# Four units of v ahead of the last down products, none between the maxima

## What is computed

```python
x = x + attn(layernorm(x))        # 16 heads of 16 channels, causal, rotary on q and k
    # q, k, v = h @ Wq.T, h @ Wk.T, h @ Wv.T ; softmax(q k^T / 4) v ; @ Wo.T
x = x + ffn(layernorm(x))         # silu(gate) * up, then down (hidden 768, integer weights)
x = x + wkv6(layernorm(x))
x = x + ffn(layernorm(x))
```

## Time and profile before

| | us |
|---|---|
| median of 3 runs | 3179.18 |
| lowest, highest | 3177.82, 3183.08 |
| the profiled execution's own time | 3171.1 |
| its span, first to last instruction | 3169.0 |
| mean granted TensorE clock, share of full speed | 0.958 |

### The profile page before, as it was taken

The page is one execution under the profiler, slowest core; times in us unless marked ns, Lnnn a source line. Parts: engine busy times, 40 slices in busy tenths (PEclk is TensorE's granted clock), DMA queues, the critical chain, the costliest instruction groups (busy, mean ns, idle before and its releaser), DMA issues.

```text
span 3169.0 us, 46787 instructions
## 1 busy us (share of the span) xinstructions
PE 2786.1 (88%) x16704; PEld 1732.4 (55%) x16704; DVE 2412.7 (76%) x4581; ACT 1420.5 (45%) x3073; POOL 1439.7 (45%) x1638
## 2 busy tenths in 40 slices
PE   4598989998899998989889998898988989899898
PEld 2235674366644576345763556635565355753667
DVE  7577887777786787867878678786787868877666
ACT  1373434744256433654336542375513744247342
POOL 2134662445624565244643357334563345623464
PEclk7799999999999999999999999899999999999999
DMA  6500143000520125001340012400124001240000
GB/s 161 123 2 9 33 68 75 2 19 24 84 59 2 31 32 94 29 2 30 49 102 4 1 41 41 102 2 2 40 41 102 2 2 40 41 89 2 8 13 15
DMA packets 80135, 128.00 MB, mean 40 GB/s; under 512 B 12443, under 2 KB 66107, under 8 KB 73707
## 3 DMA queue, kind: packets, MB, share of 16 engines
q1 hardware_dynamic: 76611, 123.71, 19.1%
q10 hardware_dynamic: 3264, 0.79, 0.1%
HBM read 75.08 MB, written 33.65 MB: 34 GB/s over the span
## 4 chain that ended last, share of the span: by engine, by line
PE 51%; DVE 24%; POOL 10%; issue 6%; ACT 4%; DMA 2%; SPq 1%; DVEq 0%; POOLq 0%; ACTq 0%
PE PB L1574 7%; PE PB L1505 6%; PE PB L1489 6%; DVE mxp L1141 6%; PE PB L1475 6%; PE PB L1589 5%; DVE arena L1344 4%; DVE arena L1353 3%; PE PB L1671 3%; POOL rstd L597 2%; PE PB L1765 2%; PE PB L1682 2%; PE PB L1426 2%; POOL hl L700 2%; PE PB L1448 2%
## 5 line engine op out<-in xcount | busy, mean ns | idle before, releaser
L853 ACT ACTIVATE arena<-PB 128x512 f32<-128x512 f32 (+3 forms) x1536 | 658.7, 511 | 403.1 <-PE PB L1489 344.4
L1141 DVE TENSOR_REDUCE mxp<-PB 128x1 f32<-128x512 f32 (+3 forms) x1216 | 723.2, 652 | 144.6 <-PE PB L1478 78.9
L1489 PE MATMUL PB<-arena 99*128 99x512 bf16 (+3 forms) x1536 | 443.9, 335 | 69.7 <-DMA arena<-augT 39.8
L1475 PE MATMUL PB<-arena 96*128 96x512 bf16 (+3 forms) x1536 | 458.2, 340 | 50.0 <-DMA arena<-parts 30.7
L700 POOL TENSOR_TENSOR hl<-arena,hh 128x512 fp32r<-128x512 f32 x192 | 251.8, 1315 | 296.9 <-ACT hh L880 295.3
L1505 PE MATMUL PB<-arena 128*32 128x512 f32 (+3 forms) x3072 | 326.1, 498 | 8.5 <-POOL arena L676 8.5
L1475 PEld LDWEIGHTS PB<-arena 96*128 96x128 bf16 x1536 | 150.7, 99 | 279.0 <-ACT arena L853 95.8
L676 POOL TENSOR_SCALAR_AFFINE_SELECT arena<-arena 128x512 f32<-128x512 f32 x256 | 162.7, 638 | 305.4 <-ACT arena L853 275.6
L1489 PEld LDWEIGHTS PB<-arena 99*128 99x128 bf16 x1536 | 138.7, 98 | 288.2 <-DVE mxp L1141 86.0
L1765 PE MATMUL PB<-arena 128*128 128x128 f32 x1792 | 247.0, 292 | 54.9 <-DVE arena L1344 45.7
L1574 PE MATMUL PB<-xh,wgu 128*128 128x512 f32 x768 | 258.4, 418 | 39.2 <-issue 36.0
(11 more groups left out here) (151 smaller groups left out, 5382.7 us busy)
## 6 DMA issues: line engine op xcount, KB each, us to landing
arena<-parts SPq DMA_DIRECT2D x112, 256.0 KB, 10.6
parts<-arena SPq DMA_DIRECT2D x192, 128.0 KB
arena<-parts SPq DMA_DIRECT2D x16, 768.0 KB, 17.9
arena<-in_x SPq DMA_DIRECT2D x16, 512.0 KB, 7.4
arena<-parts SPq DMA_DIRECT2D x16, 512.0 KB, 19.8
xres<-in_x SPq DMA_DIRECT2D x16, 512.0 KB, 4.8
mix_in<-lora_hi SPq DMA_DIRECT2D x128, 64.0 KB, 2.0
out<-xres SPq DMA_DIRECT2D x16, 512.0 KB, 11.8
```

The lines of the kernel that those rows point to most:

```text
L853: act.activation(pt[:, U % 3, h, 0:n], bank(b, "score", t)[:, 0:n], ACT.Exp, scale=DH ** -0.5).then_inc(act_emptied, 1)
L1141: dve.reduce_max(mxp[:, k // 2 % 2, hs[0]:hs[-1] + 1, col:col + 1], bank(b, "max", t)[:, 0:n * len(hs)].rearrange("p (h n) -> p h n", n=n) ...
L1475: last = mm(ps, qst[0:AUG, i // 4, HG * (k // 2) + h, 128 * (i % 4):128 * (i % 4) + 128], kst[0:AUG, s0 // HALF, HG * (k // 2) + h, 0:n], ...
L1489: mm(ps[:, 0:n], kst[0:AUG + 3, j // 4, h, 128 * (j % 4):128 * (j % 4) + 128], qst[0:AUG + 3, f, h, HALF - n:HALF], start=True, stop=True) ...
```

## The change

The plan and PE's list both get all four units of v ahead of the last down products of the second FFN, and in the prologue ahead of the first maximum. The two units at steps 4 and 8 of the maxima are gone. Nothing else is edited: the same products, copies and reductions are done, and ACT's, DVE's, POOL's and SyncE's lists are unchanged.

```diff
-V_AT = (4, 8)
@@ psum_plan, ffn
         elif b + 1 < NB:
-            add(b + 1, "v", (0, 1), "act")
+            add(b + 1, "v", range(4), "act")
         add(b, f"dn{k}", (2, 3), "dve")
@@ psum_plan, prologue
-    add(0, "v", (0, 1), "act")
+    add(0, "v", range(4), "act")
@@ psum_plan, steps of the attention
-            if t in V_AT:
-                add(b, "v", (2 + V_AT.index(t),), "act")
@@ PE, prologue
-                v_item(0, 0)
-                v_item(0, 1)
+                for n in range(4):
+                    v_item(0, n)
@@ PE, steps of the attention
-                        if t in V_AT:
-                            v_item(b, 2 + V_AT.index(t))
@@ PE, ffn
                         elif ahead:
-                            v_item(b + 1, 0)
-                            v_item(b + 1, 1)
+                            for n in range(4):
+                                v_item(b + 1, n)
                         for n in (2, 3):
                             down(n, 0, (NM - 1,))
```

## The result

The changed kernel takes 3217.3 us (median of 4, 3212.98 to 3218.59) against 3181.13 for the kernel before (4 runs): a ratio of 1.0107, 95% interval 1.009 to 1.0124. It is slower by 36.2 us. The direction was forecast; the size was not: 3198.9 was predicted, 19.7 us slower, and 3217.3 lies above the stated range.

A forecast was written before the change was run, and what follows sets the result against it. The prediction took the chain of waits through the seam, then DVE's pace in the maxima, as the bound. Per seam +3.45 + 0.48 - 1.12 = +2.81 us; seven seams, +19.7 on 3179.18, gave 3198.9 us, range 3191 to 3208.

The forecast's parts named there:

- The seam, +3.45: Between sequences, ahead of the last down products: two more units of v delay these by their whole length, +3.45 us a seam.
- the banks of `dn3`: Down products at the seam: `dn3` 2 and 3 wait for later gate and up banks, covered by POOL's low part; cost nothing.
- Rival (b): At the seam: the new units hide in a wait that ends later than read; 3174.7 us, chance 0.03.
- The new wait ahead of the first maximum, +0.48: Behind the seam: maximum 0 waits for ACT to copy v out of its bank, so DVE starts +0.48 us later a seam.
- What comes back between the maxima, -1.12: Among the first maxima: removing two units returns only DVE's idle 0.30 and 0.82 us, since DVE sets the pace; -1.12 a seam.
- Rival (a): Between the maxima: PE's relief comes back in full, 3.56 us a seam instead of 1.12; 3181.8 us, chance 0.06.
- All that follows (maxima, splits, scores) hangs on DVE's progress, so the 1.12 is carried forward: From the first maxima through the scores: DVE's progress sets the pace, so the 1.12 us gained a seam is kept.
- nothing else could use the 3.45 us: At the seam: DVE, ACT and POOL idle until `dn3` banks are filled, so the added 3.45 us serve no other work.
- The first sequence, nothing: In the first sequence, added units and DVE's gain both vanish in waits for transfers of 30.70 and 33.52 us; no change.
- Zero for the clock: Behind the seam: the clock falls earlier, its effect between -3.5 and +4.5 us in all, taken as zero.
- Rival (c): Behind the seam: the clock falls early and is still down when scores and maxima share PE; 3206.8 us, chance 0.13.
- the sign that the prediction gave for (c): Behind the seam: a longer time from first maximum to first join would show the clock returning late; before, 23.2 to 24.4 us.

The follow-up runs named there:

- late_before: Kernel before the change, plus a SyncE wait: loads of the next x start only once the first `augT` transfer has landed; ratio 0.9982 to before, 0.999 repeated.
- late_after: Changed kernel, plus a SyncE wait: loads of the next x start only once the first `augT` transfer has landed; ratio 1.0025 to before, 1.0032 repeated.
- before_again: Kernel before the change, nothing edited, run for a second profile; 3181.94 us (one run).
- spread_stack_late: Against spread: second-half head loads wait for the first `augT` transfer to land, loads of x for the second; 3216.55 us, ratio 1.0091 to the kernel before.
- spread: Against the kernel before: no unit of v at the seam, all four between the maxima at steps 6, 11, 15, 20; 3146.02 us, ratio 0.9894.

## Why the prediction was wrong

**The seam, +3.45: right.** 16.61 became 20.04, +3.43, at every seam. PE was not idle ahead of the last down products, and the banks of `dn3` cost nothing. Rival (b) is out.

**The new wait ahead of the first maximum, +0.48: right,** 0.58 measured, and no idle time behind it.

**What comes back between the maxima, -1.12: right as a mechanism.** The two idle times are gone, and with the loads held back the way to the join is 0.65 us shorter (24.52 and 24.56 in the late_before pair, 23.88 and 23.87 in the late_after pair), where 0.48 - 1.12 = -0.64 was forecast. Rival (a) would have had 2.4 us more there.

**"All that follows (maxima, splits, scores) hangs on DVE's progress, so the 1.12 is carried forward": this step failed.** Between the maxima and the first score stands a transfer, and it hangs on what else is in flight. The text of the prediction had weighed the engines at the seam and written that nothing else could use the 3.45 us. The transfer engines could: they drained the head loads, and the loads of x arrived 2.8 us earlier relative to T than before. The rows were at hand: PE's wait of 0.82 us for `augT` stood in the timeline before, the loads of x 0.8 us ahead of `augT`, and at the first and the fourth seam the chain went through it. I took DVE's unbroken 12.70 us as proof that the wait had no price, and did not ask how far it was from having one. Where PE waited 3.73 us DVE idled 2.41, so 1.3 us of a wait were covered (1.4 in before_again, 4.53 against 3.11); the change took the wait from 0.82 to 3.73.

**The size.** Over the two profiles of each kernel, the way to the join is 25.88 after and 24.76 before: +1.12 where -0.64 was forecast. That is 7 x 1.76 = 12.3 of the 16.5 us that the prediction lacked. The remaining 4 us (7.5 by the spans of these profiles) are spread over other stages. In the profile after, the way from the first to the second join is 1.1 us longer in three of eight sequences, one of them the first, which has no seam ahead of it; in the two profiles before this happened once. At the two seams among them the granted clock is at 0.50 a second time, from T + 28.8 to T + 32.4, and at no other seam of that profile. The last stretch of the first FFN is 0.4 us longer on average. I have not tied these to the transfers by a run of their own; they went when the loads of x were put late.

**The first sequence, nothing: not contradicted.** Its first join comes 122.0 and 125.1 us into the two profiles before, and 124.0 and 122.7 into the two after.

**Zero for the clock: right at the seam, not elsewhere.** The granted clock fell earlier, at T + 8.4 to T + 9.0 instead of T + 11.7 to T + 14.1, as forecast, and was back at T + 22.0 to T + 22.7, where before it came back between T + 18.8 and T + 22.4. Rival (c) wanted it back later behind the first maximum than the 19 to 23 us of before; it was back after 20.7 to 21.4. Yet the sign that the prediction gave for (c), a longer time from first maximum to first join, did come: 24.67 and 24.55 us after against 23.70 and 24.35 before. The sign did not tell the clock from the transfers. late_after does: with the same early fall and the loads held back this time is 22.60, against 23.79 in late_before, and the forecast 1.12 is there. (The spread that priced (c) was also misread: the largest of the seven before is 24.44 at the fifth seam, not 24.34.) But the pair without the meeting of transfers is 12.8 us apart, not the 2.79 x 7 = 19.5 of its seams. The untouched stages account for the rest, and somewhat more: 8 x 0.64 + 7 x 0.40 = 7.9 us less. Their rows differ in the granted clock. At the fifth sequence of late_before and of late_after, at the last stretch of the first FFN:

```profile
1827.20:1829.20 2.00, 0.61 (x3) 0.64 (x4) 2.00 (x3) 0.63 (x1) 2.00 (x3) 0.83 0.00 0
1829.20:1831.20 2.00, 2.00 (x11) 2.00 (x11) 1.33 (x3) 0.00 (x0) 0.53 (x1) 0.50 0.00 0
```

```profile
1841.00:1843.00 2.00, 2.00 (x18) 2.00 (x18) 1.86 (x3) 0.00 (x0) 1.06 (x1) 1.00 0.00 0
```

In the two late_before profiles the clock fell a second time there in two sequences of eight, at 1.4 us each; in the two late_after profiles in none. Why this differs within the pair, some 180 us behind the seam, stays open.

The Trainium skill, "DMA: Bandwidth & Descriptors", section "Queues, rings and completion order", bears on the failed step: SyncE and ACT own separate queues on the same 16 engines, and a transfer's semaphore increment lands only after every earlier write of that engine, across its queues. By that rule the signal of a small transfer in ACT's own queue would wait for SyncE's bulk ahead of it. The traces show such waiting: 2.3 us with nothing ahead, 5.4 behind the last head loads and the stores, 6.8 with x0 just ahead, 11.9 amid the head loads. But in the 6.8 us it is not the signal that waits. The packets of `augT` themselves do not move for 5.2 us, against 1.35 in late_after. What holds the packets back is not shown.

## What to carry to other kernels

When work is added to a stage during which transfers run, list the transfers as one more engine: the stream goes on, and all that is issued behind it comes earlier relative to the end of the stage. A small transfer on the path should be issued ahead of bulk loads that nobody waits for soon; one wait on SyncE gave back 24 to 29 of 36 us here. And take a wait that is hidden now by its distance from mattering, over more than one profile: here 1.3 us of cover, and waits of 0.4 to 4.5 us in executions of the same kernel.

## What the runs showed of the hardware that was not expected

- A transfer of 12 KB took from 2.3 to 11.9 us from issue to landing, by what another queue had in flight. At the second seam after the change none of its packets moved for 5.2 us, while SyncE's queue moved 1.46 MB.
- At 1.2 GHz PE kept DVE busy 7.91 of 8.00 us in maxima and first scores: where another engine set the pace, 3.5 us more at half clock went with 0.3 to 0.5 us more to the join.
- With four units of dense products spread among the maxima, as in spread_stack_late, the clock stayed at 1.00 for 24 us behind T at all seven seams, where it fell in every seam of the kernel before. In spread it still fell within 18 us of T at two of seven.
